# Cross-attention on one core: first pairs back on the steady order, one moments instruction on a third transfer of the rows, and the fourth query rows on VectorE

## The reference

```python
mu = jnp.mean(input, axis=(1, 2), keepdims=True)
var = jnp.var(input, axis=(1, 2), keepdims=True)
xn = (input - mu) * rsqrt(var + EPS) * gamma + beta
q = einsum('oc,ncs->nos', Wq, xn) + bq            # 8 heads of 64
kv = einsum('od,nds->nos', Wkv, context) + bkv    # keys and values
att = softmax(einsum('nhqc,nhkc->nhqk', q * scale, k * scale), axis=-1)
y = einsum('nhqk,nhkc->nhqc', att, v)
out = einsum('co,nos->ncs', Wo, y) + bo
return input + out
```

## Time and profile before

| | us |
|---|---|
| median of 3 runs (728.31 to 729.72) | 728.36 |
| the profiled execution | 729.8 |
| its span, first to last instruction | 728.0 |
| busy: PE, DVE, ACT, POOL | 671.5, 676.2, 620.7, 566.8 |

### The profile page before, as it was taken

One profiled execution on the slowest core, in us unless ns is written; L12 is line 12 of the kernel. 1 busy time (PEld: TensorE's weight loads), 2 busy tenths in 40 slices (PEclk: granted clock), 3 DMA queues, 4 the chain that ended last, 5 costly groups with the idle time before them and its releaser, 6 DMA issues.

```text
span 728.0 us, 29894 instructions
## 1 busy us (share of the span) xinstructions
PE 671.5 (92%) x11268; PEld 448.2 (62%) x11268; DVE 676.2 (93%) x1124; ACT 620.7 (85%) x2248; POOL 566.8 (78%) x360
## 2 busy tenths in 40 slices
PE   7995999999999999999999999999999999989986
PEld 6763666566666656666665666665666666656654
DVE  1895999999999999999999999999999999999993
ACT  2885888899888889988889988889998888988883
POOL 2784688788888878888887888888788888778863
PEclk7997999999999999999999999999999999999999
DMA  5202222222222222222222222222222222222110
GB/s 123 52 26 75 71 55 67 75 74 72 74 59 61 68 70 70 70 70 65 58 68 70 70 72 65 63 62 70 70 70 75 58 59 70 73 73 59 47 46 23
DMA packets 74823, 47.68 MB, mean 65 GB/s; under 512 B 33748, under 2 KB 74708, under 8 KB 74772
## 3 DMA queue, kind: packets, MB, share of 16 engines
q1 hardware_dynamic: 72450, 46.46, 23.9%
q10 hardware_dynamic: 2322, 0.53, 0.4%
HBM read 25.96 MB, written 4.19 MB: 41 GB/s over the span
## 4 chain that ended last, share of the span: by engine, by line
PE 59%; DVE 19%; issue 8%; SPq 8%; ACT 3%; DMA 1%; POOLq 0%; POOL 0%; ACTq 0%; DVEq 0%
PE z L466 29%; PE fill L432 24%; DVE neg_max L621 9%; DVE probs_t L634 7%; SPq L346 6%; PE z L477 3%; ACT probs L561 3%; PE z L491 1%; DVE y L677 1%; DVE spread L665 1%; SPq L298 1%; DMA x_res<-in_x 1%; SPq L309 1%; DMA bq_col<-in_L_xattn_bq 1%; DVE recip L627 1%
## 5 line engine op out<-in xcount | busy, mean ns | idle before, releaser
L722 POOL TENSOR_TENSOR probs<-probs,recip 128x1024 f32<-128x1024 f32 x256 | 482.4, 1895 | 132.3 <-DVE recip L627 131.4
L561 ACT ACTIVATE probs<-fill,neg_max 128x256 f32<-128x256 f32 x1024 | 473.6, 488 | 80.1 <-DVE neg_max L621 77.2
L621 DVE TENSOR_REDUCE neg_max<-fill 128x4 f32<-128x1024 f32 x256 | 307.5, 1202 | 16.9 <-PE fill L432 15.5
L634 DVE STREAM_TRANSPOSE probs_t<-probs 128x1024 f32<-128x1024 f32 x256 | 310.6, 1222 | 2.9 <-POOL probs L722 0.9
L432 PE MATMUL fill<-c,t 64*128 64x256 f32 x2048 | 285.9, 400 | 28.6 <-ACT probs L561 25.4
L432 PEld LDWEIGHTS fill<-c,t 64*128 64x128 f32 x2048 | 185.0, 187 | 117.3 <-ACT probs L561 84.9
L466 PE MATMUL z<-probs_t,ctx_keys 32*64 32x256 f32 x8192 | 254.5, 381 | 1.8 <-DVE y L677 1.3
L561 ACT ACTIVATION_READ_ACCUMULATOR probs<-fill,neg_max 128x1 f32 x1024 | 225.0, 220 | 0.0
L466 PEld LDWEIGHTS z<-probs_t,ctx_keys 32*64 32x64 f32 x8192 | 174.9, 131 | 67.7 <-issue 35.4
L570 ACT ACTIVATE t<-z,d_col 128x512 f32<-128x512 f32 x128 | 88.4, 741 | 5.4 <-PE z L444 5.4
L577 ACT COPY z_sb<-z 128x1024 f32<-128x1024 f32 x64 | 62.0, 1034 | 7.3 <-PE z L466 7.3
(11 more groups left out here) (42 smaller groups left out, 132.0 us busy)
## 6 DMA issues: line engine op xcount, KB each, us to landing
ctx_keys<-ctx_turned SPq DMA_DIRECT2D x512, 32.0 KB, 1.9
x<-in_x SPq DMA_DIRECT2D x64, 128.0 KB, 2.8
c<-in_ctx SPq DMA_DIRECT2D x64, 128.0 KB, 2.7
ctx_rows<-in_ctx SPq DMA_DIRECT2D x128, 32.0 KB, 1.8
x_res<-in_x SPq DMA_DIRECT2D x32, 128.0 KB, 2.3
out<-y SPq DMA_DIRECT2D x32, 128.0 KB, 1.8
wq<-in_L_xattn_Wq ACTq DMA_DIRECT2D x2, 128.0 KB
wv<-in_L_xattn_Wkv SPq DMA_DIRECT2D x2, 128.0 KB
```

Source lines behind the costliest of these rows:

```text
L561: ins = act.activation(probs[:, k % SLOTS, g, :], bank[:, K * qt:K * qt + K], ACT.Exp, bias=neg_max[:, k, g:g + 1], accum_out=denom[:, k, ...
L621: dve.tensor_reduce(neg_max[:, k, :], fill[k % PAIRS_OF_BANKS][:, :, :].rearrange("p o (t k) -> p (o t) k", t=QT), AX.X, ALU.max, negate=T ...
L634: dve.transpose(probs_t[p][:, s, :, :, hp, :, :].rearrange("p b o t j -> p o t b j"), probs[:, k % SLOTS, :, :].rearrange("p (o t) (b j) - ...
L722: pool.tensor_tensor(p, p, recip[:, k, :].unsqueeze(2).broadcast_to([128, 2 * QT, K]), ALU.mult).then_inc(probs_ready, 1)
```

## The change

It has four parts.

1. **Third transfer.** `load_x` first loads the pair's rows once more, with both samples' channels over the 128 partitions, into a new buffer `x_rows` (two of them). One `bn_stats` over it takes the place of the two. `mean_var` and `spread` write the halves of tiles whose other halves are zero, and the two tiny matmuls sum over 128 partitions instead of 64.
2. **`t` 3 on VectorE.** The fourth query rows' instruction goes from ACT to DVE (`last_query_rows`, with a semaphore of its own). Its place on DVE is behind `max` 7.
3. **Orders.** All tables have new times. On SP the order of a steady round was `store`, `spread_context`, `load_ct`, `load_x`, `residual`, `load_c`; it is now `store`, `load_x`, `spread_context`, `load_ct`, `residual`, `load_c`. On DVE `turn_context` goes from behind `sample_var` to behind `recip` 1, `turn` 5 from the round's end into the next one, `moments` to ahead of `max` 0.
4. **First pairs.** The tables of pairs 0, 1, 2 have the steady times, with two exceptions: `moments` of pair 1, and `residual` of pairs 0 and 1, which stands in the pair's own round at 1.50. The warm-up of PE is 13, 4 and 1 matmuls at three places instead of 12 at one.

```diff
-WARM_UP = 12
+WARM_UP = (13, 4, 1)
 DVE_ORDERS steady
-             + at('turn_context', 1.89) + at('result', 32.35)),
+             + at('turn_context', 6.32) + at('result', 32.03) + at('t', -0.46)),
 SYNC_ORDERS steady
-    STEADY: (at('load_x', -8.74) + at('load_c', 14.57) + at('load_ct', 2.69) + at('spread_context', 2.49)
-             + at('residual', 24.35) + at('store', 32.85)),
+    STEADY: (at('load_x', -9.19) + at('load_c', 14.69) + at('load_ct', 7.12) + at('spread_context', 6.92)
+             + at('residual', 24.03) + at('store', 32.53)),
+    0: (at('load_x', -9.19) + at('load_c', 14.69) + at('load_ct', 7.12) + at('spread_context', 6.92)
+        + at('residual', 1.50) + at('store', 32.53)),
...
             def load_x(pair, row):
                 p = pair.parity()
+                sync.dma_start(x_rows[p][:, :], x[bass.ds(row, PS), :, :].rearrange("s c q -> (s c) q")
+                               ).then_inc(x_rows_loaded[p], 16)
...
+            def last_query_rows(pair):
+                hp = HP - 1
+                wait(dve, projected, pair.count(HP // 2, HP // 2))
...
+                dve.tensor_scalar(t[pair.parity()][:, hp, :, :], z[:, hp, :], d_col[:, hp:hp + 1], None, ALU.add
+                                  ).then_inc(t_last_ready, 1)
...
             def channel_moments(pair):
                 p = pair.parity()
-                wait(dve, x_loaded[p], pair.dma_count(1) * 2)
-                for s in range(PS):
-                    dve.bn_stats(moments[:, s, :], x2[p][:, s, :]).then_inc(moments_ready, 1)
+                wait(dve, x_rows_loaded[p], pair.dma_count(1))
+                dve.bn_stats(moments[:, :], x_rows[p][:, :]).then_inc(moments_ready, 1)
...
-                    dve.bn_aggr(mean_var[:, s, :], moments[:, s, :]).then_inc(mean_var_ready, 1)
+                    dve.bn_aggr(mean_var[64 * s:64 * s + 64, s, :], moments[64 * s:64 * s + 64, :]).then_inc(mean_var_ready, 1)
```

More of the change, by code:

```diff
@@ L46 @@
 PE_ORDERS = {
[L47 to L59, removed]
+    STEADY: (at('scores', 0.00, 1.27, 3.48, 5.69, 7.21, 10.11, 10.87, 13.69)
+             + at('mix', 18.03, 18.79, 20.24, 21.00, 22.45, 23.97, 24.74, 25.42) + at('project_out', 30.37)
+             + at('project_in', -4.40, -3.67) + at('mean', -16.22) + at('var', -15.22)),
@@ L60 @@
+    2: (at('scores', 0.000, 1.270, 3.480, 5.690, 7.210, 10.110, 10.870, 13.690)
+        + at('mix', 18.030, 18.790, 20.240, 21.000, 22.450, 23.970, 24.740, 25.420) + at('project_out', 30.370)
+        + at('project_in', -4.400, -3.670) + at('mean', -16.220) + at('var', -15.220)),
 }
 ACT_ORDERS = {
[L62 to L65, removed]
@@ L70 @@
+    1: (at('exp', 1.930, 3.760, 5.520, 7.620, 9.380, 12.210, 14.420, 15.790) + at('t', -2.430, -2.000, 1.160)
+        + at('z', 26.740, 27.480)),
+    2: (at('exp', 1.930, 3.760, 5.520, 7.620, 9.380, 12.210, 14.420, 15.790) + at('t', -2.430, -2.000, 1.160)
+        + at('z', 26.740, 27.480)),
 }
 DVE_ORDERS = {
[L72 to L75, removed]
-             + at('turn_context', 1.89) + at('result', 32.35)),
@@ L77 @@
[L77 to L91, removed]
+    STEADY: (at('max', 0.98, 2.81, 4.56, 6.67, 8.42, 11.09, 12.95, 14.71)
+             + at('recip', 3.64, 6.26, 8.36, 9.26, 11.03, 13.79, 15.97, 17.89)
+             + at('turn', 7.50, 9.32, 10.18, 12.10, 13.85, 17.95, 19.70, 21.40) + at('moments', -31.35)
+             + at('mean_var', -20.07) + at('spread', -15.66) + at('sample_var', -14.19)
+             + at('turn_context', 6.32) + at('result', 32.03) + at('t', -0.46)),
@@ L92 @@
+    2: (at('max', 0.980, 2.810, 4.560, 6.670, 8.420, 11.090, 12.950, 14.710)
+        + at('recip', 3.640, 6.260, 8.360, 9.260, 11.030, 13.790, 15.970, 17.890)
+        + at('turn', 7.500, 9.320, 10.180, 12.100, 13.850, 17.950, 19.700, 21.400) + at('moments', -31.350)
+        + at('mean_var', -20.070) + at('spread', -15.660) + at('sample_var', -14.190)
+        + at('turn_context', 6.320) + at('result', 32.030) + at('t', -0.460)),
 }
 POOL_ORDERS = {
-    STEADY: (at('divide', 4.65, 6.75, 8.33, 9.74, 11.15, 13.87, 15.63, 18.38) + at('root', -12.21)
-             + at('norm', -14.90, -9.94)),
@@ L264, in build @@
         t_ready = sem("t_ready")
+        t_last_ready = sem("t_last_ready")
         scored = sem("scored")
```

93 lines of the change are left out of this document (67 added, 26 removed).

## The result

The changed kernel takes **851.05 us** (median of 5 runs, 848.92 to 852.11) against 728.36 (5 runs as well, 728.00 to 729.72): a ratio of 1.1674, with a 95% interval of 1.1652 to 1.1696. It is 16.7% slower; 836 us was forecast (816 to 862). The profiled execution took 849.11 us with a span of 847.3.

A forecast was written before the change was run, and what follows sets the result against it. DVE bounds the kernel before, but SP's late `x_res` would bound the changed one. Result 1 at 79.5 + 657.8 for 26 rounds + 9.0 + 51.0 + 23.2 + 12.15 + 2.7 = 835.4 us span, forecast 836 us, range 816 to 862.

The forecast's parts named there:

- The mechanism: SP's steady round: `x_res`, issued behind the 16 `spread_context` transfers, lands at 25.3 us; `result` waits, rounds 25.3 instead of 21.42.
- 8.96 against 10.3: Steady round, us behind `result`: `turn_context` done at 8.96, SP's sample loads issued until 10.3, so the loads hold up the 16 transfers.
- The sum: Whole kernel: result 1's start, the rounds and the end add to 835.4 us of span; median 836 us.
- Start: First pairs: 7.49 us of DVE idle time go; `project_in` of pair 0 maybe 1.9 us; result 0 at 58.0, result 1 at 79.5.
- The 26 rounds: Intervals up to results 2 to 27: 25.3 us each, 657.8 together, plus 1.5 us for each of six.
- The end: Last rounds: 2 x 25.5, 23.2 and 12.15 us, then 2.7 from the last result's start to the span's end.
- The landing: `x_res` from issue to arrival: issued at 22.8, landing at 25.1 by the median or 25.6; 25.3 taken.
- The clock's rival: PE's clock falls each round while `result` waits; `turn_context` moves to 11.3, costing 1.0 us a round: 862 us; chance 0.13.
- "Both at nothing" for `moments` and `t` 3: DVE: `moments` 0.33 us less, `t` 3 some 0.6, net about +0.3 a round, costed at nothing under 3.9 us of idle time.
- The shorter wait: Rival: SP is through with the loads and starts the 16 transfers at 8.96; round 24.0 us, 802 us in all; chance 0.08.
- `x_res` in time: Rival: the 16 transfers issue 4 us or more faster, `x_res` arrives before 21.4, rounds stay 21.42; 716 us; chance 0.04.
- The low end of the range: Whole kernel: 25.1 - 0.4 us a round and no surcharge for unrolled rounds: 836 - 16 - 4 = 816 us.

The follow-up runs named there:

- run with the residual early: Changed kernel with one number changed: `residual` of every pair at 1.50 in its own round, ahead of the 16 transfers; 741.85 us, ratio 1.0181.
- run with the busy PE: Changed kernel plus eight 128x128 matmuls whose results are not used, behind the first `scores` item of each pair from 3 on; 840.28 us, ratio 1.1526.
- run at full width: Changed kernel with `residual` early in every pair, and `mean_var` and `spread` over all 128 partitions instead of halves, mixing both samples' statistics; 728.35 us, ratio 0.9981.

## Why the prediction was right, and where a term was mis-sized

*The mechanism was right.* `x_res` stands behind the 16 transfers, these wait until 10 us and more behind the result, each round hangs on the one before, and nothing is caught up. The run with the residual early shows it, by 109 of 123 us. That `turn_context` and the loads each suffice was seen in the working (8.96 against 10.3) and is shown by the runs that undo one. That the loads alone decide the start of the 16 was right for one round of two: in the others the falling clock makes `turn_context` the later one.

*The sum came out 12 us short of the span* (835.4 against 847.3), in three places. Of the median's error of 15 us the other 3 come from the profiled execution, which I had taken to lie 1.4 us above the median; here it lies 1.9 below.

- Start, 3.3 us: result 1 starts at 82.78, not 79.5. `max` 0 of pair 0 came early enough (17.64 against 19.02 before). The fill behind it was mis-sized: 43.1 us to result 0, where before had 40.6 from `max` 0 to the end of its work at 59.6. The first pairs run in the steady order now, and no run undoes that order, so how much of the 2.5 us it takes is open. The clock falls there too, to 0.50 in the window 34 to 36, where it was 1.00 before:

```profile
34.00:36.00 2.00, 2.00 (x8) 0.93 (x6) 2.00 (x4) 2.00 (x8) 0.04 (x1) 0.50 0.20 49
```

  The fewer pauses that I expected for `project_in` were not enough either: 3.41 us, not 1.9.
- The 26 rounds, 7.4 us. The six up to results 2 to 5, 26 and 27, which are unrolled rounds and the first of the loop, take 160.8 us, just the 6 x 26.8 forecast. The other 20 take 25.67 instead of 25.3.
- The end, 1.3 us: 27.00 + 26.01 + 21.62 + 13.03 instead of 25.5 + 25.5 + 23.2 + 12.15. In the first two no sample loads stand ahead of the 16 transfers, and these start with the end of `turn_context`, as forecast; but it is done at 11.0 and 11.2 us, not at 8.96. In the run with the busy PE the second has it at 8.85 and takes 24.22.

*Inside the round* two terms were off to the late side and one to the other. `max` 0 starts at 1.80, not 1.42, since `spread` in halves takes 0.60 instead of 0.37 and `moments` 0.55 instead of 0.44; so `xhat` is done at 8.56 to 8.65, not 8.13. I had said that such costs are hidden under the wait. They are not: what stands ahead of the event that SP waits for is on the path, however long DVE idles later. The landing takes 2.1 us, not the 2.5 that I allowed. Together they give the 25.29 of the run with the busy PE. That this meets the 25.3 forecast is luck: `x_res` is issued there at 23.0 and 23.4 by turns, not at 22.8, and the landing that was put too long makes up for it.

*The clock's rival was half right.* It gave `turn_context` at 11.3 where the clock falls; 11.14 was measured. The clock falls in all rounds from result 2 to 28, but early enough to matter in every second one, and there only 0.65 us are paid, not the 1.0 in each round that the rival had. Over the kernel the busy PE gave back 11 us by the medians and 8.7 by the profiled executions, and most of my error is this. I had set it aside with "a fall late in the pause is hidden", which holds for one round of two. I had said that a clock below 0.9 in the loop would make the forecast wrong; it was 0.90.

*"Both at nothing" for `moments` and `t` 3* holds roughly for the total, since the wait covers most of it, and not for the instructions: the round with the residual early is 0.65 us longer than before's 21.42, where +0.3 less 0.38 of idle time was given. `t` 3 was sized well (0.65 from start to start). Missing were the two pairs in halves, 0.37 us a round by the run at full width, whose 21.70 is before's round plus 0.28; and the idle time did not go to DVE's new work (by the busy times of eight rounds it is still 0.30 us a round). Undoing `t` 3 alone gives 0.20 of it back, the statistics alone 0.05, both 0.13; the 0.52 that remain come with the new order, in which the two idle times named above stand.

*The shorter wait and `x_res` in time* did not come: in the loop the 16 transfers took 10.1 us from whatever start. The 716 us of the second holds more than the 7.5 and 1.6 us that it names: it also puts before's longer rounds, 23.49 up to result 1 and 22.41 up to result 27, at 21.42.

*The low end of the range was summed wrongly.* Without any surcharge for the nine unrolled rounds 13.5 us go, and 4 were taken off; by its own terms it lies at 806 or below, not at 816. The measured time is near the other end, so this decided nothing.

## What to carry to other kernels

Where a queue issues its transfers in order, follow for each of them what it stands behind and when that may start; a short transfer that the bounding engine needs belongs ahead of a long series that waits for something else. An edit priced at nothing because of a later idle time must be checked for what stands between it and the event that ends that idle time. When a change has a good part and a bad one, run the good part alone: a gain of 0.7 to 0.9% at the start lay under 17% of loss in the loop.
